# Low-rank products of two weight tiles as one set, in two halves, in a fused feed-forward kernel

## What is computed

```python
x = x + ffn0(conv(x, cond, weight, c_weight, bias), ...)     # grouped conv, then quantized FFN with low-rank parts
x = x + moe(mix(x, cond, ...), gate_w, gate_b, expert_w, expert_b)   # per-sample mixing, then top-1 of 8 experts

# ffn0, the part that the change is in; H = 2752, D = 1024, R = 16, NF4 = table of 16 values, one scale per 64 weights
w_up = (NF4[w_up_codes] * repeat(w_up_absmax, 64)).reshape(H, D).T
y1 = x1 @ w_up + b_up + x1 @ w_up_lora_a @ w_up_lora_b
x2 = relu(y1)
w_down = (NF4[w_down_codes] * repeat(w_down_absmax, 64)).reshape(D, H).T
y2 = x2 @ w_down + b_down + x2 @ w_down_lora_a @ w_down_lora_b
```

## Time and profile before

| | |
|---|---|
| median of 3 runs | 1503.43 us (1503.21 to 1505.74) |
| profiled execution | 1503.95 us, its span 1502.5 us |
| mean granted TensorE clock | 0.973 |
| TensorE busy (products) | 1421.0 us, 95% |
| VectorE busy | 1125.3 us, 75% |
| ScalarE busy | 759.4 us, 51% |
| DMA | 227 GB/s over the span |

### The profile page before, as it was taken

How to read it: one execution, slowest core, us unless ns; L and a number is a source line. 1 busy time by engine, 2 the same in 40 slices (tenths; PEclk the granted TensorE clock), 3 DMA queues, 4 the chain that set the end, 5 groups by cost and what they waited for, 6 DMA issues and landing times.

```text
span 1502.5 us, 20838 instructions
## 1 busy us (share of the span) xinstructions
PE 1421.0 (95%) x6815; PEld 1168.3 (78%) x6815; DVE 1125.3 (75%) x1075; ACT 759.4 (51%) x845; POOL 181.9 (12%) x214
## 2 busy tenths in 40 slices
PE   6886999999999999999999999999999679999996
PEld 5676878888888888888888888888885468888785
DVE  3662788788888778788788778778234689999895
ACT  3561544644644544644644644644103167777673
POOL 0112200000000000000000000000001044466461
PEclk8898999999999999999999999999999879999998
DMA  5567467556656647556556546556644855878961
GB/s 166 201 208 284 180 234 259 219 199 252 226 194 262 229 184 269 208 207 256 206 208 256 224 188 269 213 198 240 232 193 177 310 154 160 291 238 265 335 193 28
DMA packets 104364, 331.29 MB, mean 220 GB/s; under 512 B 17360, under 2 KB 24920, under 8 KB 104248
## 3 DMA queue, kind: packets, MB, share of 16 engines
q1 hardware_dynamic: 80478, 258.22, 46.0%
q0 software_dynamic: 22512, 71.32, 15.0%
q10 hardware_dynamic: 1298, 0.68, 0.2%
HBM read 295.04 MB, written 46.14 MB: 227 GB/s over the span
## 4 chain that ended last, share of the span: by engine, by line
PE 89%; DVE 3%; DMA 3%; ACT 2%; issue 1%; ACTq 0%; POOL 0%; SPq 0%; DVEq 0%; POOLq 0%
PE pair L1071 26%; PE pair L1073 26%; PE pair L1072 26%; PE pair L1120 3%; PE pair L1215 2%; DMA am<-am_dn 2%; PE pair L1280 1%; DMA batch_kernels<-aggs 1%; PE pair L1130 1%; DVE wf L775 1%; PE pair L1222 1%; PE pair L1133 1%; PE pair L1230 1%; PE pair L1116 1%; PE pair L1104 0%
## 5 line engine op out<-in xcount | busy, mean ns | idle before, releaser
L775 DVE TENSOR_TENSOR wf<-wf,term 128x1024 f32<-128x1024 f32 x308 | 377.1, 1224 | 93.5 <-ACT term L568 74.7
L568 ACT ACTIVATE term<-codes 128x1024 f32<-128x1024 int32 x308 | 321.0, 1055 | 107.0 <-DVE wf L775 107.0
L1071 PE MATMUL pair<-wh,hh 128*128 128x512 f32 x704 | 275.5, 391 | 3.9 <-DVE acc L814 2.5
L1073 PE MATMUL pair<-wh,hl 128*128 128x512 f32 x704 | 275.0, 391 | 0.0
L1072 PE MATMUL pair<-wl,hh 128*128 128x512 f32 x704 | 274.9, 391 | 0.0
L814 DVE TENSOR_TENSOR acc<-acc,pair 128x1024 f32<-128x1024 f32 x176 | 214.2, 1217 | 57.9 <-PE pair L1073 57.8
L1071 PE MATMUL pair<-ring,wh 128*128 128x512 f32 x656 | 255.8, 390 | 1.3 <-issue 1.3
L1073 PE MATMUL pair<-ring,wl 128*128 128x512 f32 x656 | 255.5, 390 | 0.0
L1072 PE MATMUL pair<-ring,wh 128*128 128x512 f32 x656 | 255.5, 390 | 0.0
L708 ACT ACTIVATE whr<-wraw 128x1024 fp32r x184 | 187.9, 1055 | 88.1 <-PE pair L1073 44.2
L1046 DVE TENSOR_TENSOR wlr<-wraw,whr 128x1024 fp32r<-128x1024 f32 x184 | 213.7, 1218 | 14.0 <-ACT whr L708 13.6
(11 more groups left out here) (165 smaller groups left out, 1414.7 us busy)
## 6 DMA issues: line engine op xcount, KB each, us to landing
ring<-x_parts SPq DMA_DIRECT2D x320, 512.0 KB, 7.8
wraw<-exp_w SPq DMA_DIRECT2D x64, 512.0 KB, 13.8
x_parts<-stage POOLq DMA_DIRECT2D x24, 512.0 KB, 8.4
xg<-exp_b POOLq DMA_DIRECT2D x23, 512.0 KB, 7.9
codes<-codes_up SPq DMA_DIRECT2D x22, 512.0 KB, 7.8
codes<-codes_dn SPq DMA_DIRECT2D x22, 512.0 KB, 6.7
am<-am_dn SPq DMA_DIRECT2D x22, 512.0 KB
acc<-x_nat POOLq DMA_DIRECT2D x16, 512.0 KB, 10.6
```

What stands on the lines that cost most here:

```text
L568: return nc.scalar.activation(out, codes[:, n % 2], ACT.Relu, scale=scale, bias=-scale * bend)
L775: nc.vector.tensor_tensor(whole(n), whole(n), term[:, e % 2], op).then_inc(term_added, 1)
L1071: mm(ps, ah, bh, start=first, stop=False)
L1073: return mm(ps, al, bh, start=False, stop=last)
```

## The change

The two up tiles of a unit in the loop (n >= 4, n % 4 = 0 and 1) no longer have a set of eight 128-column products each. Their operands lie side by side in `lora_t`, and one set of eight products of 256 columns serves both: each product yields one 128-row block of the input dimension for both tiles. `pair[1]` holds only four of them, so the set is made in two halves. Half 0 stands where the set of the second up tile stood (`down` of the pass with k % 4 = 1, between quarters 1 and 2), half 1 inside the next pass's `up`, after its second kt (k % 4 = 2). In the pass with k % 4 = 0 there is no low-rank product any more.

VectorE adds each half to both tiles in one operation of 1024 elements (`add_half`): half 0 where `add_lora` stood in the pass with k % 4 = 1, half 1 in the pass k % 4 = 2 after ramp 2. `high` and `low` of both up tiles move to the pass k % 4 = 2: `high` twice after ramp 3 on ScalarE, `low` after ramp 3 and after ramp 4 on VectorE. `lora_high` of the pass k % 4 = 2 now waits for half 1 of the same pass. The first unit's tiles (n < 4, before the loop) are made as before.

```diff
             def lora_high(i, n):
                 act.wait_ge(lora_in, i * 128 + 16 * (n + 1))
-                wait(act, ab_mm, i * 8 + n - 1)
+                wait(act, ab_mm, i * 8 + n - (n % 4 != 2))
                 nc.scalar.activation(lora_t[:, n % 2], lora_raw[:], ACT.Copy).then_inc(lora_high_ready, 1)
             def high(i, n):
-                act.wait_ge(w_ready, i * 8 + n + 1)
+                act.wait_ge(w_ready, i * 8 + n + 1 + (n >= 4 and n % 4 == 0))
...
-                    if not early:
+                    if not early and k % 4 in (0, 3):
                         high(i, k + 3)
                     lora_high(i, k + 4)
                     head(i, k + 4)
-                    ramps(i, k + 4, range(1, 7))
+                    ramps(i, k + 4, range(1, 4))
+                    if k % 4 == 2:
+                        high(i, k + 2)
+                        high(i, k + 3)
+                    ramps(i, k + 4, range(4, 7))
...
             def add_lora(i, n):
+                if n >= 4 and n % 4 < 2:
+                    if n % 4 == 1:
+                        add_half(i, n, 0)
+                    return
...
+            def add_half(i, n, h):
+                dve.wait_ge(ab_mm, i * 8 + n + h)
+                dve.wait_ge(scaled, i * 8 + n + 1)
+                both = wf[:, n // 4 % 2, 0:2, h * 512:(h + 1) * 512].rearrange("p s (c n) -> p s c n", n=P)
+                nc.vector.tensor_tensor(both, both, pair[1][:].rearrange("p (c s n) -> p s c n", c=4, n=P),
+                                        ALU.add).then_inc(w_ready, 1)
...
                         add_ramps(i, k + 4, (1,))
-                        low(i, k + 3)
+                        if k % 4 in (0, 3):
+                            low(i, k + 3)
                         lora_low(i, k + 4)
-                        add_ramps(i, k + 4, range(2, 7))
+                        add_ramps(i, k + 4, (2,))
+                        if k % 4 == 2:
+                            add_half(i, k + 3, 1)
+                            add_ramps(i, k + 4, (3,))
+                            low(i, k + 2)
+                            add_ramps(i, k + 4, (4,))
+                            low(i, k + 3)
+                            add_ramps(i, k + 4, (5, 6))
+                        else:
+                            add_ramps(i, k + 4, range(3, 7))
                         hidden_low(i, k + 1)
...
+            def lora_pair(i, n, h):
+                if h == 0:
+                    pe.wait_ge(lora_ready, i * 8 + n + 1)
+                wait(pe, w_ready, i * 8 + n - 1 + h)
+                for c in range(4):
+                    ins = mm(pair[1][:, c * 2 * P:(c + 1) * 2 * P], lora[:, (4 * h + c) * P:(4 * h + c + 1) * P],
+                             lora_t[:].rearrange("p s n -> p (s n)"), start=True, stop=True)
+                ins.then_inc(ab_mm, 1)
+
             def lora_product(i, n):
+                if n >= 4 and n % 4 < 2:
+                    if n % 4 == 1:
+                        lora_pair(i, n, 0)
+                    return
...
-            def up(i, q, between=None):
+            def up(i, q, between=None, halves=None):
...
+                    if kt == 1 and halves:
+                        lora_pair(*halves, 1)
...
-                    up(i, k + 1).then_inc(up_mm, 1)
+                    up(i, k + 1, halves=(i, k + 3) if k % 4 == 2 else None).then_inc(up_mm, 1)
```

## The result

The changed kernel takes 1536.89 us (median of 4 runs, 1530.74 to 1546.14) against 1503.41: ratio 1.0208, 95% interval 1.0172 to 1.0243. **Slower, as forecast, but by 33 us and not by 14, and outside the range.** The profiled execution took 1536.64 us (span 1535.2). It is 32.7 us longer than the profiled one of before, and its runs scatter over 15 us where the four of before scattered over 3.

A forecast was written before the change was run, and what follows sets the result against it. TensorE, busy 95% of the span, was taken as the bound. Nine pairs at +1.70 us (-0.90 - 0.43 + 0.47 + 2.55) and a first pair at -1.0 gave +14.3 us: 1518 us, range 1510 to 1526.

The forecast's parts named there:

- Products: Low-rank products on TensorE: two halves of 0.47 us replace two sets of 0.90 us, saving 0.86 us a pair.
- rival B: The weight load is not hidden behind a 256-column product: 8.6 us less saved, 1527 us; chance 0.03.
- The wait behind the copy: Passes k % 4 = 2: copy L592, head and ramps start late, so TensorE waits 2.55 us for L814.
- The first pair: In the first pair TensorE's old wait for L814 goes, 2.69 us: -1.0 us for that pair.
- Rival A: The wait at the copy L592 costs nothing and TensorE does not wait: 1493 us, faster; chance 0.08.
- rival C: The stall lets the clock fall to half for the two quarters behind: 10 x 2.7 us more, 1545 us; chance 0.04.
- The jumps: At the loop's jumps back TensorE waits three times, 1.3 us together, in the kernel before; no change was forecast.

The follow-up runs named there:

- e1: The changed kernel with a third buffer for the low-rank operand of passes k % 4 = 2, so its copy needn't wait: 1504.65 us, ratio 0.9999 to before.
- e4: The changed kernel with head and ramps 1 and 2 ahead of the waiting copy on ScalarE, lora_low behind ramp 2 on VectorE: 1500.50 us, ratio 0.9978 to before.
- e3: The kernel before with four idle VectorE additions (three of 1024 elements, one of 512) in passes k % 4 = 2, to make a stall: 1534.77 us, ratio 1.0215.
- e6: The kernel before with 32 semaphore increments a round, which nobody waits for, in TensorE's stream: 1509.99 us, ratio 1.0014.
- e7: The kernel before with three idle VectorE additions of 1024 elements in passes k % 4 = 2, a smaller made stall: 1532.54 us.
- e8: The kernel before with four idle VectorE additions of 1024 elements in passes k % 4 = 2, a longer made stall: 1543.15 us.
- filled: The changed kernel with 34 semaphore increments a round, which nobody waits for, put into TensorE's stream: 1532.90 us.
- e2: The changed kernel with one of the two low operations of passes k % 4 = 2 moved behind the first accumulator addition: 1536.11 us.
- e5: The head-first kernel with 34 semaphore increments a round, which nobody waits for, put into TensorE's stream: 1501.82 us, ratio 0.9957 to the kernel before.

## Why the prediction was wrong, and where it was right

- **Products:** right. A half costs 0.48 us to the next product, 0.51 with the tail (0.47 taken), an old set 0.94 with its tail, so a pair saves 0.87 (0.86 worked out). The weight load is hidden behind 256 columns: 0.120 us a product from start to start, so rival B is out. The Trainium skill's rule as the prediction cites it (TensorE: Matmul & The Clock Gate, Part 3, The mechanism) would give the 0.214 estimated there, and the trace disagrees; the same section also lets a load for the background weight buffer go ahead of products in flight, which the prediction left out and which fits the 0.120.
- **The wait behind the copy:** right in place, releaser and size. 2.62 us a pair with the tail against 2.55, no later pass waits (one pause in the loop's first pass, see the first pair), and e1 and e4 show its cause. Rival A was wrong about the kernel as changed and right about what a different order gives: with head first it is this rival's schedule, 89.07 us for four passes.
- **The first pair:** nearly right, -0.2 us instead of -1.0 (a pause of 0.82 us in the loop's first pass is new there).
- **The clock:** the step that failed. The prediction took the one pause of 2.5 us at 187 us with clock 1.00 as a sign that a pause of this size does no harm, and gave rival C 0.04. One pause without a fall doesn't say so when ten are coming: the same pause stands in five traces (before, e3, e6, e7, e8), and in one of them, e7, the clock fell behind it. Of the ten stalls seven and six brought a fall in the two traces of the changed kernel and four in e3. C's price was wrong too, in the other direction: 1.6 to 1.7 us for a fall (once 3.2), not 2.7, and not behind every stall: 13.1 us, not 27.
- **The jumps:** a term left out. The prediction told of three jumps and of 1.3 us there and never asked what fewer instructions do to them: 3.6 us in the changed kernel.
- The forecast without these two terms was 14.3 us against 15.6 measured; with 13.1 for the clock and 3.6 for the jumps that is the loop's 32.3. The change was slower for the reason given; its range lacked C, which alone reaches 1531 at the measured price.
- Open: what decides whether a stall brings a fall. The changed kernel had 7, 6 and (filled) 6 of 10, e3 with nearly the same stalls 4 of 10, but e2, which has the changed products and stalls of 2.6 to 2.9 us, also 4 of 10. So the changed products are not shown to matter, and with ten stalls to a trace neither is the difference. That the two traces of the changed kernel fell at nearly the same stalls speaks for the position in time; no run tests it.

## What to carry to other kernels

When a wait is added on an engine, price the instructions queued behind it in program order, and look whether one of them can go ahead: here three instructions moved past a copy of 0.3 us turned 33 us more into some 3 less (ratio 0.9978, 0.9957 to 0.9999). Stalls of TensorE of 2.5 to 3.3 us, in a kernel that otherwise runs it nearly without a gap, cost more here than themselves, because the granted clock fell behind about half of them; one such pause at full clock in the old trace is no assurance. In a hardware loop, taking instructions out of an engine's stream can lengthen the pause at the jump (here from 0.7 to 0.9 us to about 2), so read that pause in the trace after every change.

## What the hardware showed that was not expected

- Pauses of TensorE from start to start, and falls of the clock from 0.8 us before to 1.4 us after their end in the loop: made stalls of 1.4 to 1.9 us (e7), 0 of 10; 2.5 to 2.8 us with no product changed (e3), 4 of 10; 2.6 to 2.9 us with one low moved (e2), 4 of 10; 2.7 to 3.1 us in the changed kernel, 7, 6 and (filled) 6 of 10; 3.1 to 3.3 us (e8), 6 of 10. Behind the jumps' pauses of 1.9 to 2.4 us, 2 of 15; behind the old pause of 2.8 us, 1 of 5.
- Inert semaphore increments inside TensorE's stream cost nothing away from the jumps (e6: the other passes are as long as before, to 0.1 us). At the jumps they shortened the pause from 2.2 to about 1.0 us where as many instructions had been taken out (e5), and cost 0.5 to 0.6 us a jump where none had (e6).
- Kernels without any fall in the loop of their profiled execution still scatter by 10 to 16 us from run to run (the one before: 1498.9 to 1510.4, and 1500.4 to 1514.8), so a gain of 0.4% needed 12 runs to be seen.
